# Moving small work between the engines and steps of tiles 0 and 1 in a fused attention and ternary feed-forward layer

## What is computed

```python
x = L0_attn_x
x = x + layernorm(attn(layernorm(x), W_qkv, W_out, b_out))
x = x + layernorm(ffn(layernorm(x), W_up, W_gate, W_down))

def attn(x, W_qkv, W_out, b_out):
    q, k, v = qkv projections, by heads
    q = q * cos + rotate_half(q) * sin
    k = k * cos + rotate_half(k) * sin
    mask = (j <= i) & (j >= i - 128)
    return softmax(where(mask, q k^T / sqrt(32), min)) v, joined, @ W_out + b_out

def ffn(x, W_up, W_gate, W_down):
    # each W: clip(round(W / mean|W|), -1, 1) * mean|W|
    return (silu(x Wu^T) * (x Wg^T)) Wd^T
```

## Time and profile before

| | us |
|---|---|
| median of 3 runs | 1301.25 |
| lowest, highest | 1299.35, 1301.84 |
| profiled execution | 1299.7 |
| its span | 1297.6 |
| PE busy | 1276.8 |
| DVE busy | 906.8 |
| ACT busy | 786.0 |
| POOL busy | 701.9 |

### The profile page before, as it was taken

How to read it: one execution, slowest core, us unless ns; L and a number is a source line. 1 busy time by engine, 2 the same in 40 slices (tenths; PEclk the granted TensorE clock), 3 DMA queues, 4 the chain that set the end, 5 groups by cost and what they waited for, 6 DMA issues and landing times.

```text
span 1297.6 us, 27066 instructions
## 1 busy us (share of the span) xinstructions
PE 1276.8 (98%) x9284; PEld 848.9 (65%) x9284; DVE 906.8 (70%) x2419; ACT 786.0 (61%) x1444; POOL 701.9 (54%) x956
## 2 busy tenths in 40 slices
PE   9889999999999999999999999999999999999998
PEld 6667666666666666666666666666666666766775
DVE  7878987767777777777777777777777668644333
ACT  4797877666556665556665665656656547633332
POOL 2766766546653656537645376544674365425432
PEclk9999999999999999999999999999999999999999
DMA  8857448657866577755868577676867647610000
GB/s 297 249 163 214 141 134 151 136 118 164 153 150 129 113 157 147 172 118 114 176 146 173 96 156 161 136 152 121 159 123 149 124 97 138 125 34 26 25 17 33
DMA packets 383815, 174.74 MB, mean 135 GB/s; under 512 B 313664, under 2 KB 363072, under 8 KB 383680
## 3 DMA queue, kind: packets, MB, share of 16 engines
q1 hardware_dynamic: 383104, 172.49, 60.2%
q10 hardware_dynamic: 576, 0.52, 0.2%
HBM read 71.76 MB, written 25.17 MB: 75 GB/s over the span
## 4 chain that ended last, share of the span: by engine, by line
PE 91%; DVE 3%; ACT 2%; DMA 2%; issue 1%; SPq 0%; ACTq 0%; DVEq 0%
PE J L1690 29%; PE Y L1708 16%; PE J L1625 15%; PE J L1635 8%; PE J L1611 6%; PE S L1690 5%; PE O L1595 4%; PE S L1562 3%; PE J L1616 1%; PE Y L1570 1%; DMA turned<-parts 1%; DMA W<-in_w_qkv 1%; ACT prob L1085 1%; PE S L1559 1%; DVE prob L1343 0%
## 5 line engine op out<-in xcount | busy, mean ns | idle before, releaser
L1708 PE MATMUL Y<-down_q,room 128*128 128x512 fp8e4 x1024 | 262.2, 379 | 0.6 <-DVE room L1408 0.6
L1625 PE MATMUL J<-xnT,W 128*128 128x512 f32 x512 | 241.0, 596 | 2.2 <-DVE xnT L1334 1.4
L1085 ACT ACTIVATE prob<-prob,peak 128x256 f32<-128x256 f32 (+1 forms) x512 | 226.6, 492 | 18.0 <-DVE peak L1343 17.7
L1343 DVE CUSTOM_DVE_ANT_0 prob<-S,band,neg_score_scale 128x256 f32<-128x256 f32 (+1 forms) x512 | 221.3, 470 | 8.0 <-PE S L1559 2.8
L1395 DVE SCALAR_TENSOR_TENSOR room<-room,J 128x512 f32<-128x512 f32 x111 | 76.3, 687 | 206.7 <-ACT room L1142 206.7
L1690 PE MATMUL J<-xT,up_q 128*128 128x256 f16 x1776 | 212.0, 273 | 0.0
L1690 PE MATMUL J<-xT,gate_q 128*128 128x256 f16 x1760 | 210.2, 273 | 0.2 <-DVE room L1395 0.2
L1142 ACT ACTIVATE room<-J,sig_scale 128x512 f32<-128x512 f32 x111 | 76.0, 685 | 219.4 <-PE J L1690 219.4
L1690 PEld LDWEIGHTS J<-xT,up_q 128*128 128x128 fp8e4 x1776 | 173.6, 98 | 43.4 <-DVE room L1402 0.2
L1690 PEld LDWEIGHTS J<-xT,gate_q 128*128 128x128 fp8e4 x1760 | 171.6, 98 | 44.4 <-DVE room L1395 2.9
L932 POOL TENSOR_TENSOR o_n<-o_raw,rinv 128x128 f32<-128x128 f32 x128 | 52.3, 408 | 254.3 <-DVE o_raw L1369 254.2
(11 more groups left out here) (172 smaller groups left out, 1936.5 us busy)
## 6 DMA issues: line engine op xcount, KB each, us to landing
spill<-split SPq DMA_DIRECT2D x64, 256.0 KB, 2.6
Qp<-spill SPq DMA_DIRECT2D x127, 128.0 KB, 2.8
Kp<-spill SPq DMA_DIRECT2D x125, 128.0 KB, 3.0
x_in<-in_x SPq DMA_DIRECT2D x32, 256.0 KB, 3.6
X<-in_x SPq DMA_DIRECT2D x32, 256.0 KB, 3.4
out_x<-X SPq DMA_DIRECT2D x32, 256.0 KB, 3.4
turned<-parts SPq DMA_TRANSPOSE x198, 3.2
Kc<-Kp SPq DMA_DIRECT2D x24, 128.0 KB, 3.7
```

The costliest lines, as they stand in the source:

```text
L1085: e = nc.scalar.activation(prob[:, prob_home(U), a, begin:], prob[:, prob_home(U), a, begin:], ACT.Exp, bias=peak[:, prob_home(U), a:a + 1 ...
L1343: e = nc.vector.tensor_tensor_reduce(out=prob[:, prob_home(U), a, begin:], in0=S_ps[U % 2][:, a * 2 * P + begin:(a + 1) * 2 * P], in1=band ...
L1625: e = pe.matmul(dst[:], W[:, part, c, g * P:(g + 1) * P], xnT[:, c, :], start=(c == 0), stop=(c == DC - 1))
L1708: e = pe.matmul(Y_ps[t][:], h[:, q % HELD, part, (a * HT + t) * P:(a * HT + t + 1) * P], down_q[:, 2 * pair + a, :], start=(pair == 0 and ...
```

## The change

- The first Q: after DVE's cosine product and swap, POOL takes the sine product and the add, directly behind the maximum over partitions. The first K stays on DVE, with a swap buffer of its own (`swap_k`, in `y_sb`, unused until tile 1); its sine product waits for POOL's, its add for POOL's add. On ACT the third absolute sum comes behind the high halves of Q and K and the first V.
- Tables of tile 0 and 1: sums, loads and signs move as shown.
- Statistics of tile 1's input at steps 8, 9, 11, 13 instead of 7 to 10; the moments at 13 instead of 10; `rstd_of_x` at 14 instead of 12, POOL's layer norm at 15 to 18 instead of 14 to 17. The loads of tile 2's input begin a step later.
- Where T jobs end (steps 19, 20, 51, 52), ACT makes the high half ahead of the copies. In steps 22 and 23 DVE makes the low half ahead of the Q or K that ends there.
- `SPLIT_X`, for tiles 3 to 7.

```diff
-          13, 14, 17, 22, 23, 24, 25, 27,
+          14, 17, 22, 23, 24, 25, 27, 28,
...
-           26, 28, 35, 37, 41, 43, 45, 47]
+           28, 30, 35, 37, 41, 43, 45, 47]
...
-UP_SIGNS = [8, 9, 10, 11, 12, 16, 18, 21]
+UP_SIGNS = [8, 9, 10, 11, 13, 16, 21, 22]
+X_STATS = [8, 9, 11, 13]
...
+LOW_FIRST = (22, 23)
...
-SPLIT_X = [11, 13, 15, 17]
+SPLIT_X = [11, 12, 14, 16]
...
+        swap_k = y_sb[:, 0, :]
...
-                first_load = 22 if i else 27
+                first_load = 22 if i else 28
...
                 pool.wait_ge(swap_done, n)
-                if i == 0:
+                if n == 1:
+                    pool.wait_ge(table_in, 32)
+                elif i == 0:
                     pool.wait_ge(tables_scaled, 2)
...
             pool.partition_all_reduce(wmax_all[:], wmax[:], P, bass.bass_isa.ReduceOp.max).then_inc(wmax_spread, 1)
+            times_sin(0, 0, 0)
+            add(0, 0, 0)
...
-                begin = 11 if i else 14
-                if u == begin - 2 and i + 1 < NM:
+                begin = 11 if i else 15
+                if u == (9 if i else 14) and i + 1 < NM:
                     rstd_of_x(i + 1)
...
             rotated_high(("Q", 0, 0))
-            absolute_sum(2)
             rotated_high(("K", 0, 0))
             empty(("V", 0, 0))
+            absolute_sum(2)
             absolute_sum(3)
...
+                turns = any(job[0] == "T" for job in ENDS[s])
+                if turns:
+                    p_high(s - 1)
                 for job in ENDS[s]:
                     empty(job)
-                for U in high_units(s):
+                for U in high_units(s) if not turns else ():
                     p_high(U)
...
-                    at_least(dve, rot_done, 2 * n + a)
+                    if n:
+                        at_least(dve, rot_done, 2 * n + a)
                     nc.vector.tensor_tensor(rot[:, a, :], bank[:], cosT[:], ALU.mult).then_inc(cos_done, 1)
...
+                    pairs = swap_k if n == 0 and a else swp[:]
+                    nc.vector.stream_shuffle(pairs, bank[:], [d ^ 1 for d in range(HD)]).then_inc(swap_done, 1)
+                    if n == 0 and a:
+                        dve.wait_ge(swap_done, 2)
+                        dve.wait_ge(sin_done, 1)
+                        nc.vector.tensor_tensor(swap_k, swap_k, sinT[:], ALU.mult).then_inc(sin_done, 1)
+                        dve.wait_ge(cos_done, 2)
+                        dve.wait_ge(sin_done, 2)
+                        dve.wait_ge(rot_done, 1)
+                        nc.vector.tensor_tensor(rot[:, a, :], rot[:, a, :], swap_k, ALU.add).then_inc(rot_done, 1)
...
+                if s in LOW_FIRST:
+                    p_low(s - 1)
                 for job in ENDS[s]:
                     empty(job)
-                for U in high_units(s):
+                for U in high_units(s) if s not in LOW_FIRST else ():
                     p_low(U)
...
-                    begin = 4 if i else 7
-                    if begin <= u < begin + TT:
-                        layer_norm_stats(i + 1, u - begin)
-                    if u == begin + (4 if i else 3):
+                    slots = range(4, 4 + TT) if i else X_STATS
+                    for t in range(TT):
+                        if u == slots[t]:
+                            layer_norm_stats(i + 1, t)
+                    if u == (8 if i else X_STATS[-1]):
                         layer_norm_moments(i + 1)
```

## The result

The change makes the kernel slower: 1309.93 us (median of 4 runs, 1309.14 to 1311.17), beside 1301.55 us for the kernel before on the same chip. The ratio is 1.0068, 95% interval 1.0052 to 1.0083. The prediction said 1298.0 with a range up to 1303.5: both are missed. The profiled execution has a span of 1307.7 us, 10.1 more than before.

The account below looks back on a forecast made before the run. PE, busy 98% of the span, was taken as the bound, leaving only the 20.8 us it stands still. Terms -0.8 - 0.7 - 0.5 + 0.5 - 0.7 - 1.0 = -3.2 us gave a median of 1298.0, range 1295.0 to 1303.5.

Parts of the forecast that it names:

- 1, the first rotation: Set-up before the first score: with POOL rotating Q, K ends 1.3 us earlier, of which PE gains 0.8.
- Rival A: At the first rotation, the switch behind the maximum holds POOL by R; 1301.4 at R = 3.9, 1303.5 at 6; chance 0.27.
- `SPLIT_X`: Split copies from tile 3 on: set at 0, because PE was said to wait for nothing there.
- 2, statistics: Tile 1's input statistics moved to later steps: DVE's sums reach PE's weighted values earlier, -0.7 us.
- 3, ACT at the first turning: ACT in tile 0: moved sign pass gains 1.0, high half ahead of the copies costs 0.5; net -0.5 us.
- 4, the second turning: Tile 1's end, steps 51 and 52: nothing leaves ACT, so high half first delays the next Q, +0.5 us.
- 5, low halves first: Steps 22 and 23: DVE makes the low half in its idle time, all behind it 0.67 earlier, -0.7 us.
- rival B: In 60:80 relief on one engine is taken back at the next; only terms 1, 6 and 4 count, 1300.0; chance 0.20.
- 6, the queue: Step 26: with a down-weight load moved behind tile 1's K packs, PE's wait of 1.1 there shrinks, -1.0 us.

Follow-up runs that it names:

- probe_switch: The kernel before with three unread POOL operations behind the maximum over partitions: a small add, the same maximum again, a small add; no total time given.
- even_splits: The kernel before with `SPLIT_X` = 10, 12, 14, 16 in place of 11, 13, 15, 17; 1298.47 us, ratio 0.9983.
- rotation_and_splits_back: The change with its first rotation undone and `SPLIT_X` back to 11, 13, 15, 17; 1297.38 us, ratio 0.9971 to the kernel before.
- more_keep_busy: The change with 30 more unread dummy products ahead of the first score; 1312.62 us, ratio 1.0093.
- high_first_once: rotation_and_splits_back with ACT's high half ahead of the copies only in steps 19 and 20, not 51 and 52; 1296.69 us, ratio 0.9969.
- splits_alone: The kernel before with only the new `SPLIT_X` = 11, 12, 14, 16; 1303.51 us, ratio 1.0022.
- late_neighbours: The kernel before with `SPLIT_X` = 11, 13, 15, 16, so only the last two copies are in neighbouring steps; 1299.10 us, ratio 0.9991.

## Why the prediction was wrong, step by step

**1, the first rotation: -0.8 said, +6.8 and +2.2 of clock measured.** The step that failed is "I take none", for the hold of POOL behind the maximum: it was bounded correctly (0 to 9.6), its real size was 8.6, and the value was taken from the nearest row, the first such switch, "at most 3.9". That row was no switch of the same kind: only fills had run on POOL before it, and not the maximum over partitions. The row that bears on it was the other one, an idle of 9.64 that could hide everything. In the probe POOL stood for 6.63 us on the way into the maximum and 9.45 and 7.54 on the way out, so the hold came again the second time. Rival A named the place and the hold; at its far bound it had "about 1307". That this is near the 1309.9 measured is partly luck: with the R of 8.6 its formula gives about 1306, and the rest is the clock and `SPLIT_X`, which it didn't have. It was given 0.27, and the range was cut off at R = 6, a figure that no row supported as an upper end. No run shows a hold of 6 us either: the four measured are 6.6 to 9.5.

Rival A's price lacked the second cost: PE's idle time grows with R, and the clock was at half when PE went on after 7.88 us. In the kernel before, the clock is 1.00 in all windows up to 1292 us; it falls once, at the very end, after PE's last product (0.98 in 1292:1294, 0.50 in 1294:1296). That row has no price, but it was a warning for a case in which PE stands for 8 us.

**`SPLIT_X`: 0 said, +3.0 measured** (2.2 and 2.4 in the two comparisons by themselves). This is the second step that failed. "PE waits for nothing there" wasn't true of before: PE waits 1.4 us there for `xnT`, which the edit took away, and which even_splits gained. And even where PE doesn't wait, that says only that nothing is to be gained. Whether something can be lost is another question: the copy in step 12 waits for a transfer issued in the step before, and DVE's `room` was ready 0.06 us ahead of PE (at 303.09 for a start at 303.15 in the kernel before).

**2, statistics: -0.7 said, -0.8 measured.** Of PE's three waits of 0.45, 0.71 and 1.15 the first is gone and the others are 0.72 and 0.80, both in the change and in rotation_and_splits_back (0.71, 0.80). Right in place and size; only the second wait didn't shrink.

**3, ACT at the first turning: -0.5 said, -0.5 measured**, by another row than the one named: the wait of 0.96 for ACT's `prob` went, and the one of 0.38 for the copies grew to 0.87. Without the high half first it is the full -1.0.

**4, the second turning: +0.5 said, +0.5 measured** (0.38 became 0.94; the wait ahead of it fell by 0.06).

**5, low halves first: -0.7 said, -0.5 measured.** The wait of 0.93 is gone, but the next, for DVE's `o_raw`, grew from 0.56 to 0.98: rival B, at one place.

**6, the queue: -1.0 said.** The wait is 0.65 in the change, -0.45; alone it was gone, -1.25 in the trace; on the median it was worth 2.0, of which the trace explains the 1.25.

So terms 2 to 6 came to -1.8 in the spans, where -2.4 was said. They are the reason why the kernel without its two bad parts is the faster one.

## What to carry to other kernels

Where an engine's order has a step that no row prices, the idle time that covers it is its bound; take the far end seriously before putting work on the critical path behind it, and let a probe of one tiny operation measure it. An edit in a stage where the bottleneck hardly waits isn't free: look at how little slack the chain had, and at what a moved step must now wait for. And a stall of TensorE can be priced twice, by its length and by the clock behind it (in the change 7.88 us, then 2.2 at a clock of 0.50).

## What was not expected of the hardware

- A switch between the maximum over partitions and POOL's plain operations held POOL 6.63 us on the way in (seen once, in probe_switch) and 7.54 to 9.45 us on the way out (8.59 in the change, 9.45 and 7.54 in probe_switch), with no row of its own in the trace.
- The granted clock fell from 1.00 to 0.50 behind waits as short as 1.3 us followed by one of 0.73 (1.30 in more_keep_busy, 1.34 in even_splits, 1.38 in high_first_once), and was back at 1.00 after 3 to 4 us; behind a wait of 1.83 us in probe_switch it didn't fall. 9.54 us of dummy products just before (more_keep_busy) did not prevent it.
- The wait ahead of tile 1's first score was between 1.10 and 3.36 us in four kernels with the same program up to it (before 1.10, splits_alone 1.72, late_neighbours 1.87, even_splits 3.36). The profile's clock rows are to be read before a difference of 2 us is put down to an edit.
